# A gate projection between the two forward time-step products, and two idle products and the spread of state 2 ahead of the first skip term

## The reference, cut to what matters

```python
xz = x @ in_proj_w.T
xs, z = jnp.split(xz, 2, axis=-1)
...
xs = jax.nn.silu(xs)
dbc = xs @ x_proj_w.T
dt = jax.nn.softplus(dbc[..., :DT_RANK] @ dt_proj_w.T + dt_proj_b)
Bm = dbc[..., DT_RANK:DT_RANK + D_STATE]
Cm = dbc[..., DT_RANK + D_STATE:]
...
dA = jnp.exp(dt[..., None] * A)
dBu = dt[..., None] * Bm[:, :, None, :] * xs[..., None]
...
y = jnp.einsum('blds,bls->bld', hs, Cm) + xs * Dvec
y = y * jax.nn.silu(z)
```

## Time and profile before

| | |
|---|---|
| median of 3 runs | 1493.72 us |
| lowest and highest run | 1484.97, 1494.01 us |
| the profiled execution, whole | 1495.54 us |
| its span, first to last instruction | 1493.7 us |
| mean granted TensorE clock | 0.937 of full speed |
| PE busy | 1262.7 us (85%) |
| DVE busy | 1200.8 us (80%) |
| ACT busy | 898.4 us (60%) |
| POOL busy | 836.4 us (56%) |

### The profile page before, as it was taken

One profiled execution on the slowest core, in us unless ns is written; L12 is line 12 of the kernel. 1 busy time (PEld: TensorE's weight loads), 2 busy tenths in 40 slices (PEclk: granted clock), 3 DMA queues, 4 the chain that ended last, 5 costly groups with the idle time before them and its releaser, 6 DMA issues. The chain is left out here.

```text
span 1493.7 us, 17449 instructions
## 1 busy us (share of the span) xinstructions
PE 1262.7 (85%) x4573; PEld 641.1 (43%) x4573; DVE 1200.8 (80%) x1388; ACT 898.4 (60%) x1247; POOL 836.4 (56%) x450
## 2 busy tenths in 40 slices
PE   3609888898998988988888989889898998888868
PEld 1307344344546434433444634434354733434343
DVE  2695799998796689999688679999779479999920
ACT  1626766766555766767464676676574676676612
POOL 3022388788152378778235258878517238878815
PEclk8859899999989889999999979999999988999979
DMA  2000112222030112222021012222103011322203
GB/s 77 14 0 2 46 71 84 85 92 77 16 113 15 31 57 86 85 86 97 17 77 66 4 58 79 91 85 86 56 1 114 16 37 65 98 85 84 85 1 127
DMA packets 30506, 92.00 MB, mean 62 GB/s; under 512 B 4790, under 2 KB 8764, under 8 KB 30428
## 3 DMA queue, kind: packets, MB, share of 16 engines
q1 hardware_dynamic: 30428, 91.10, 18.0%
HBM read 88.34 MB, written 2.75 MB: 61 GB/s over the span
## 5 line engine op out<-in xcount | busy, mean ns | idle before, releaser
L664 POOL TENSOR_TENSOR work<-expo,ring 128x1024 f32<-128x1024 f32 x128 | 300.1, 2365 | 164.4 <-DVE expo L1364 162.3
L664 POOL TENSOR_TENSOR ring<-ring 128x1024 f32<-128x1024 f32 x128 | 300.2, 2367 | 26.7 <-DVE ring L1364 26.7
L1364 DVE TENSOR_TENSOR_SCAN ring<-ring,ps 128x1024 f32<-128x1024 f32 x128 | 284.7, 2263 | 6.9 <-PE ps L1786 6.9
L1364 DVE TENSOR_TENSOR_SCAN expo<-ring,ps 128x1024 f32<-128x1024 f32 x128 | 285.6, 2270 | 0.0
L1822 PE MATMUL ps<-ring,ident 128*128 128x512 f32 x512 | 260.4, 615 | 25.5 <-POOL ring L664 18.7
L1822 PE MATMUL ps<-work,ident 128*128 128x512 f32 x512 | 241.1, 593 | 0.0
L953 ACT ACTIVATE ring<-dt_f,decay 128x1024 f32<-128x1024 f32 x128 | 147.0, 1148 | 118.9 <-DVE expo L1364 80.7
L719 ACT ACTIVATE b_dtx_tok<-dtx_tok,b_tok 128x256 f32<-128x256 f32 x448 | 189.2, 493 | 0.0
L1786 PE MATMUL ps<-ident,b_dtx_tok 128*128 128x128 f32 x896 | 121.8, 279 | 43.9 <-DVE expo L1364 40.1
L1786 PEld LDWEIGHTS ps<-ident,b_dtx_tok 128*128 128x128 f32 x896 | 96.8, 141 | 134.0 <-issue 69.2
L1822 PEld LDWEIGHTS ps<-ring,ident 128*128 128x128 f32 x512 | 83.7, 189 | 159.7 <-POOL ring L664 116.6
(11 more groups left out here) (280 smaller groups left out, 2075.6 us busy)
## 6 DMA issues: line engine op xcount, KB each, us to landing
ring<-c_rows SPq DMA_DIRECT2D x128, 512.0 KB, 3.6
b_dtx_tok<-comb_rows SPq DMA_DIRECT2D x16, 512.0 KB, 4.0
dtx_tok<-comb_rows SPq DMA_DIRECT2D x16, 512.0 KB, 4.7
x_c<-in_x SPq DMA_DIRECT2D x4, 512.0 KB, 3.3
out<-xs_f SPq DMA_DIRECT2D x4, 512.0 KB, 2.6
w<-in_L_ffn_w SPq DMA_DIRECT2D x2, 512.0 KB
ring<-in_L_attn_f_in_proj_w SPq DMA_DIRECT2D x1, 256.0 KB
ring<-in_L_attn_b_in_proj_w SPq DMA_DIRECT2D x1, 256.0 KB
```

Of the source, the lines that this page charges most:

```text
L664: pool.tensor_tensor(hc[odd][:, k, :], hs[odd][:, k, :], c_all[:, odd, :], ALU.mult).then_inc(hc_ready, 1)
L1364: v.tensor_tensor_scan(hs[odd][:, k, order], dA[:, k, order], dbu[:, order], 0.0, ALU.mult, ALU.add).then_inc(scan_ready, 1)
```

## The change

Only TensorE's program changes; no other engine's instructions or waits do. Between the two forward time-step products now stands the gate projection z (0, 1), which stood behind both. Ahead of the first skip term TensorE now waits for the third scan, runs two idle products (four MATMUL rows) into `ps23`, and makes the spread of state 2; the skip term and its wait for `dt_ready` come behind. The idle products are the only work added.

```diff
                 project_z(b, 0, 0)
                 b_rows(b, 0)
                 project_dt(b, 0, 0)
+                project_z(b, 0, 1)
                 project_dt(b, 0, 1)
-                project_z(b, 0, 1)
                 project_z(b, 1, 0)
                 dtx_to_tokens(b, 0, 0)
...
                 project_dt(b, 1, 0)
                 b_rows(b, 1)
                 project_dt(b, 1, 1)
+                pe.wait_ge(scan_ready, b * UNITS + 3)
+                keep_busy(2, ps23)
+                spread(b, 0, 2, 0)
                 pe.wait_ge(dt_ready, b * DIRS * BLOCKS + 3)
                 skip_term(0, 0)
-                spread(b, 0, 2, 0)
                 add(b, 0, 0, 0, [0])
```

## The result

| | before | changed |
|---|---|---|
| median of the runs | 1493.72 us | 1502.54 us |
| the profiled execution, whole | 1495.54 us | 1493.69 us |
| its span | 1493.7 us | 1491.9 us |
| mean granted TensorE clock in it | 0.937 | 0.947 |

The changed kernel takes 1.005 times as long as the one before, 95% interval 1.0028 to 1.0073: 4 to 11 us more. One of its nine runs, 1651.25 us at a granted clock of 0.727, is in a slow state and stands outside that ratio; the other eight lie between 1493.35 and 1505.90 us, with a median of 1499.3. The profiled execution is one of the fastest of them, while that of the kernel before took 1495.54 us and its nine runs 1484.97 to 1495.56. So the traces show how the parts moved, and how much the whole moved is taken from the ratio.

A forecast was written before the change was run, and what follows sets the result against it. It took VectorE's chain from each image's first product on as the bound. +7.3 us at the forward dt products and -3.2 us at the skip term gave +4.1, on the median 1497.8, so 1498 us; range 1486 to 1507.

The forecast's parts named there:

- The engine and the chain that decide: VectorE's chain behind `cap_step(0, 1)` is late with it; at the skip term, the chain through `add` counts, not VectorE.
- the sign of each half: z (0, 1) between forward dt products costs +7.3 us; idle products and spread ahead of the skip term give -3.2 us.
- What bounds the image: From an image's first product on, VectorE hardly waits, so shifting that product moves the end by nearly as much.
- First place, which images: At the forward dt products the clock falls in images 1 and 3 (+3.1, +3.4 us), holds in 0 and 2 (-0.4, +1.2).
- First place, the lag: The second forward cap step starts 3.4 us after the first with the clock up, 6.9 with it down.
- First place, the tail: From the second forward cap step to the first product: 6.2 us with the clock up, 7.4 at half clock.
- First place, the sum: Shift of the first products behind the forward dt products, over four images: +7.3 us, lowest -3.3, highest +13.3.
- Second place: Ahead of the skip term: spread wait goes, clock returns sooner, `add` starts 0.8 us earlier an image; -3.2 us in all.
- the clock holds in all images: Rival, chance 0.22: clock holds through both forward dt products in every image; -7.5 us, 1486 us.
- nothing matters: Rival, chance 0.05: something later in the kernel takes up the shift; 1494 us.
- Interleaving does nothing for the clock: Rival, chance 0.15: all four images pay at the forward dt products, +13.3 - 3.2, 1504 us.

The follow-up runs named there:

- the gate block alone: Kernel before with only z (0, 1) moved between the two forward dt products: median 1500.41 against 1491.83 us, ratio 1.0075.
- the last version with the block: Changed kernel plus one idle product behind z (0, 0) and two ahead of the backward dt product: 1486.98 against 1491.65 us for the kernel before, ratio 0.9971.
- the half alone: Kernel before with only the wait for the third scan, two idle products and spread of state 2 ahead of the skip term: 1486.88 against 1491.83 us, ratio 0.9961.

## Why the prediction was right, and where it was not

The forecast was no change by over 1%, 1498 us, which is +4.1; measured were a median of 1502.54 (1499.3 without the run at 1651.25) and a ratio worth 4 to 11 us. The engine and the chain that decide were foreseen, and so was the sign of each half. That the number came so near is in good part luck, as the points below show:

- *What bounds the image.* Held. The distance from the first scan of a transposed product on is the same in both traces, and the halves add within their intervals.
- *First place, which images.* Wrong: images 1 and 3 should have fallen and 0 and 2 held; it came out the other way round. The clock fell in two of four, as summed, but which ones is no property of the image. With the gate block alone images 2 and 3 fell early, in the changed kernel 0 and 2, both times. And in image 0 it fell at 159.71 although z (0, 1) had run since 158.50: that late a start of full rows did not save it.
- *First place, the lag.* 3.4 us with the clock up was somewhat short, 3.82 was measured: four passes take 1.92 us here (505.85 to 507.77), where the prediction took 1.72.
- *First place, the tail.* 7.4 us at half clock was right (172.21 - 164.86 = 7.35). 6.2 with the clock up was too short: 516.74 - 509.78 = 6.96, and 6.8 in image 3. The new idle time of 2.55 us behind z (1, 0) had been foreseen, and as what would spoil the forecast that it might let the clock fall. The clock did fall behind it, at 514.70 and 1217.85, under the transposes and the spread, in the two images in which it had held. Where it held longer, in image 2 of the last version with the block, the tail is 6.11 us and nothing waits. With the clock down, 20 us and more from z (0, 0) to the first product were too many: 18.8 and 18.1 in this trace, 19.7 to 20.5 where the clock fell earliest in the others.
- *First place, the sum.* +7.3 was forecast, as -0.4, +3.1, +1.2 and +3.4 for images 0 to 3. This trace has +5.9, as +3.6, -1.0, +4.4 and -1.1: near in sum, wrong in every image, which is luck. And the gate block alone costs 11 us by its ratio (7 to 15). The 3 to 4 us that are missing lie in the base more than in the tail: the forecast puts the first products at 62.7 + 7.3 = 70.0 us, and three traces have 70.7 on average; but 62.7 came from one late execution, and four traces with the program of before have 59.0 on average.
- *Second place.* The wait of the products for the spread is gone, and the wait ahead of the scan was to be near 1.9 us: it was 1.62, 1.68, 2.80 and 2.18. -3.2 was forecast, -3.9 came out in the trace (-1.4, -1.2, -0.7 and -0.7), and -5.8 (-7.8 to -3.9) by the ratio of the half alone, of which its trace shows 3.6 there. The clock was to come back 4.0 us after the idle products begin. In image 1 it took 3.1 (532.05 to 535.18), in the others 3.0, 5.4 and 4.2, and over the twelve images of the three traces with this half it took 2.8 to 5.7, 4.0 on average. So this term was right in its mechanism and a little small. By the ratios of the halves the sum is +5.4, by the whole +7.5: both terms were taken too small, with opposite signs, and that helped +4.1.
- *The rivals.* That the clock holds in all images fell, and so did that nothing matters. "Interleaving does nothing for the clock" has a number, 1504, that lies nearer to 1502.54 than the forecast does, and farther from 1499.3. Its mechanism is wrong: with the order of before the clock first fell 4.1 to 7.3 us after z (0, 0) began, in all 16 images of four traces; with the block between it held until 13.4 to 14.1 us in 6 of 12 images, and fell after 4.1 to 6.3 in the other six. What the rival said of the cost did come out: against the mean of those four traces every image pays, +2.8, +1.3, +5.1 and +2.6 us on average over the three with the block. The rule of the Trainium skill from which it was made ("TensorE: Matmul & The Clock Gate", section "Why this matters for your kernels": keep busy, no idle gaps) is borne out by half here, for gaps of 1.1 and 2.0 us, which are shorter than those that the page warns of: filling them brought 3 us at the first place and 6 with the second by the ratios. But busy time isn't all. TensorE was busy for 5.62 of the 6.73 us ahead of the fall in image 2 before, mostly with 16-row products, and for only 10.34 of the 14.00 us in which the clock held in image 1 after, with the full rows of z (0, 1) between the two dt products.

## What to carry to other kernels

Before putting work between two products, ask which engine's queue stands behind the second one: here VectorE's whole chain stood behind it, and to start the second cap step 3.8 us behind the first, and not 1.7, cost more than the clock that it might save. Idle matmuls paid here where they fit into time in which TensorE waits for another engine anyway, ahead of the products with few rows. Where the clock falls in other images in each execution, the trace of the kernel before is one draw as well: a forecast that is counted from it takes over its luck. The size of an effect is to be taken from several executions, and one trace only tells its place.

## What was not expected of the hardware

Four passes of 512 columns took 1.72 us in a row of their like (541.54 to 543.26 before), but 1.92 us where passes of 16 and of 128 rows alternate in fours (505.85 to 507.77 to 509.68 after), both at full clock: 0.2 us for each change of kind. Why a change costs that was not tested. And the gap of one microsecond ahead of the small products was worth filling: two idle passes there, on an engine that was idle anyway, brought 0.2% (0.9981, 0.9968 to 0.9994). With them the clock held through both dt products in 6 of 8 images, without them in 6 of 16.
